# A Mamba and mixture-of-experts kernel: one pair of y additions moved from VectorE to ScalarE and GpSimd, two small products as transposes, statistics in later slots

## The reference

```python
x = x + layernorm(mamba(layernorm(x)))
x = x + layernorm(moe(layernorm(x)))

def mamba(x):                       # 512 channels, 16 states
    x_in, z = split(x @ W_in)
    u = silu(causal_conv4(x_in) + conv_b)
    dt, B, C = split(u @ W_xproj)
    delta = softplus(dt @ W_dt + b_dt)
    h = exp(delta * A) * h_before + delta * u * B    # for each channel and state n
    y = sum over n of h[n] * C[n]
    return ((y + D_skip * u) * silu(z)) @ W_out

def moe(x):                         # 8 experts of 128, top 2; a shared one of 256
    coef = softmax(x @ router), all but the two largest set to 0
    routed = sum over e of coef[e] * ((silu(x @ gate[e]) * (x @ up[e])) @ down[e])
    return routed + (silu(x @ s_gate) * (x @ s_up)) @ s_down
```

## Time and profile before

| | before |
|---|---|
| median of 3 runs | 2335.7 us (2333.97 to 2335.87) |
| the profiled execution | 2333.0 us, its span 2331.2 us |
| granted TensorE clock, mean over the span | 0.945 of full speed |
| DVE scans (L836), 1024 | 1261.1 us busy, 1267 ns each |
| DVE y additions (L846), 896 | 621.5 us busy, 735 ns each |
| GpSimd d_bu (L1103), 512 | 1202.2 us busy, 2359 ns each |
| ScalarE decays (L633), 1024 | 699.6 us busy, 691 ns each |
| TensorE transposes of h (L465), 4096 | 607.3 us busy |
| the page's 40 slices | VectorE 9 tenths in all but the first and the last two |

### The profile page before, as it was taken

The page is one execution under the profiler, slowest core; times in us unless marked ns, Lnnn a source line. Parts: engine busy times, 40 slices in busy tenths (PEclk is TensorE's granted clock), DMA queues, the critical chain, the costliest instruction groups (busy, mean ns, idle before and its releaser), DMA issues. The chain is left out here.

```text
span 2331.2 us, 30455 instructions
## 1 busy us (share of the span) xinstructions
PE 2070.9 (89%) x9280; PEld 1347.3 (58%) x9280; DVE 2155.3 (92%) x3056; ACT 1644.8 (71%) x2488; POOL 1963.8 (84%) x1625
## 2 busy tenths in 40 slices
PE   7678989999898999989899999998989989997978
PEld 4355665656566565655656566565656656565654
DVE  4999999999999999999999999999999999998950
ACT  5656877777777676777777777777768777775632
POOL 4677998989989898998989899898988989798844
PEclk8659999999999999999999999999999999998979
DMA  5111212211122121112211121121122111111201
GB/s 144 33 44 37 71 55 60 59 55 55 56 64 64 51 68 51 56 57 63 64 51 59 60 60 55 60 59 56 50 67 61 55 60 50 55 56 46 71 20 46
DMA packets 92995, 134.28 MB, mean 58 GB/s; under 512 B 12048, under 2 KB 43024, under 8 KB 92832
## 3 DMA queue, kind: packets, MB, share of 16 engines
q1 hardware_dynamic: 92832, 132.34, 18.4%
HBM read 123.13 MB, written 9.18 MB: 57 GB/s over the span
## 5 line engine op out<-in xcount | busy, mean ns | idle before, releaser
L836 DVE TENSOR_TENSOR_SCAN h<-d_a,carry,d_bu 128x512 f32<-128x512 f32 x1024 | 1261.1, 1267 | 47.0 <-ACT d_a L633 38.4
L1103 POOL TENSOR_TENSOR d_bu<-delta_u,b_rows 128x1024 f32<-128x1024 f32 x512 | 1202.2, 2359 | 4.4 <-issue 0.2
L633 ACT ACTIVATE d_a<-delta,a_neg 128x512 f32<-128x512 f32 x1024 | 699.6, 691 | 499.0 <-DVE h L836 493.9
L465 PE MATMUL ht<-ident,h 128*128 128x128 f32 x4096 | 607.3, 293 | 100.9 <-DVE y_t L846 94.3
L465 PEld LDWEIGHTS ht<-ident,h 128*128 128x128 f32 x4096 | 503.5, 150 | 333.6 <-issue 123.3
L846 DVE SCALAR_TENSOR_TENSOR y_t<-ht,c_t,y_t 128x512 f32<-128x512 f32 x896 | 621.5, 735 | 2.2 <-PE ht L465 1.5
L540 PE MATMUL ring<-x_t,w_gate_sb 128*128 128x512 f32 x640 | 327.8, 638 | 21.7 <-ACT delta L798 17.9
L567 PE MATMUL dn<-w_down_sb,up_hidden 128*128 128x256 f32 x1280 | 302.9, 379 | 1.7 <-POOL up_hidden L1166 1.7
L547 PE MATMUL ring<-x_t,w_up_sb 128*128 128x512 f32 x640 | 292.5, 600 | 11.9 <-ACT silu_gate L732 11.8
L1161 POOL TENSOR_TENSOR up_hidden<-silu_gate,up_hidden 128x512 f32<-128x512 f32 x160 | 204.3, 1277 | 110.8 <-ACT up_hidden L736 79.6
L567 PEld LDWEIGHTS dn<-w_down_sb,up_hidden 128*128 128x128 f32 x1280 | 236.0, 190 | 60.0 <-issue 31.8
(11 more groups left out here) (127 smaller groups left out, 2029.3 us busy)
## 6 DMA issues: line engine op xcount, KB each, us to landing
b_rows<-b_rows_hbm SPq DMA_DIRECT2D x256, 256.0 KB, 3.4
coef_rows<-coef_rows_hbm SPq DMA_DIRECT2D x128, 256.0 KB, 3.5
xa<-L_attn_x_in SPq DMA_DIRECT2D x16, 512.0 KB, 5.0
xr<-L_attn_x_in SPq DMA_DIRECT2D x16, 512.0 KB, 5.1
out<-xr SPq DMA_DIRECT2D x15, 512.0 KB, 2.9
w_in_sb<-L_attn_W_in_in SPq DMA_DIRECT2D x1, 1024.0 KB, 6.3
w_gate_sb<-L_ffn_experts_gate_in SPq DMA_DIRECT2D x2, 512.0 KB, 4.9
w_up_sb<-L_ffn_experts_up_in SPq DMA_DIRECT2D x2, 512.0 KB, 5.5
```

Of the source, the lines that this page charges most:

```text
L465: last = nc.tensor.transpose(HT[q % HTS][:, j * P:(j + 1) * P], H[:, (NS * c + n) % HS, j, a * P:(a + 1) * P], IDN[:, :])
L633: nc.scalar.activation(DA[i % DAS][:, :], DL[:, r, j, :], ACT.Exp, scale=ANEG[:, j, n:n + 1]).then_inc(ex.sem, 1)
L836: nc.vector.tensor_tensor_scan(H[:, (NS * s + n) % HS, j, :], DA[(n * J + j) % DAS][:, :], BU[:, (2 * n + j // 2) % 4, j % 2, :], CARRY[:, ...
L1103: nc.gpsimd.tensor_tensor(BU[:, (2 * n + h) % 4, :, :], DU[:, 2 * h:2 * h + 2, :], BB[:, n % 2, :].unsqueeze(1).to_broadcast([P, 2, T]), A ...
```

## The change

Tiles 14 and 15 are no longer added by VectorE. ScalarE scales each into one of the two buffers `UP`, and GpSimd adds both at once to `YT`. TensorE's tiles 16 and 17 wait for the ScalarE copies (`y_side`), VectorE's tiles 18 and 19 for the sum (`y_sum`), and so do the up copies of blocks 2 and 3, which write `UP`. The matmuls with the identity of `CF_PE` and `CT_PE` become transposes. Three entries of the statistics' table move: two `bn_stats` from slots 26 and 36 to 32 and 42, `XA_MEAN` from 42 to 46.

```diff
-        scan, add_c, carry = stage("scan", NS * J), stage("add_c", (NS - 2) * NT), stage("carry_s", NS)
+        y_side, y_sum = stage("y_side", 2), stage("y_sum", 1)
+        scan, add_c, carry = stage("scan", NS * J), stage("add_c", (NS - 2) * NT - 2), stage("carry_s", NS)
-        XA_STATS, XA_MEAN, XA_RSTD, XA_NORM, XT_PE, XT_ACT = (16, 16, 26, 36), 42, 47, 50, 61, 62
+        XA_STATS, XA_MEAN, XA_RSTD, XA_NORM, XT_PE, XT_ACT = (16, 16, 32, 42), 46, 47, 50, 61, 62
+        SIDE_SLOT = 20
+        SIDE_Q = ADDS[SIDE_SLOT]
         def added(c, q):
...
+            if q in SIDE_Q:
+                return y_side.sem, y_side.at(c, q - SIDE_Q[0] + 1)
-            return add_c.sem, add_c.at(c, q - NT + 1)
+            return add_c.sem, add_c.at(c, q - NT + 1 - (2 if q > SIDE_Q[1] else 0))
...
-                        last = nc.tensor.matmul(bank[0:E, a * P:(a + 1) * P], COEF[:, a, :],
-                                                IDN[:, :], start=True, stop=True)
+                        last = nc.tensor.transpose(bank[0:E, a * P:(a + 1) * P], COEF[:, a, :], IDN[:, :])
...
-                        last = nc.tensor.matmul(ring_bank("ct", 0)[:, a * NS:(a + 1) * NS],
-                                                XD[ROW_C:ROW_C + NS, o, a * P:(a + 1) * P],
-                                                IDN[ROW_C:ROW_C + NS, ROW_C:ROW_C + NS],
-                                                start=True, stop=True)
+                        last = nc.tensor.transpose(ring_bank("ct", 0)[:, a * NS:(a + 1) * NS],
+                                                   XD[ROW_C:ROW_C + NS, o, a * P:(a + 1) * P],
+                                                   IDN[ROW_C:ROW_C + NS, ROW_C:ROW_C + NS])
...
+            def side_state(c, r, q):
+                n, a = q // NT, q % NT
+                act.wait_ge(ht_full.sem, ht_full.at(c, q + 1))
+                act.wait_ge(hf.sem, hf.at(c - 1, up_used(1)))
+                act.wait_ge(y_sum.sem, y_sum.at(c - 1))
+                nc.scalar.activation(UP[:, q - SIDE_Q[0], :], HT[q % HTS][:, :], ACT.Copy,
+                                     scale=CT[:, r, a, n:n + 1]).then_inc(y_side.sem, 1)
...
+                    if with_scan and t == SIDE_SLOT:
+                        for q in SIDE_Q:
+                            side_state(s, r, q)
...
+                        if f // 2 == 1 and exists(lo):
+                            act.wait_ge(y_sum.sem, y_sum.at(s))
                         nc.scalar.activation(UP[:, f % 2, :], ring_bank("up", f)[:, :], ACT.Copy)\
...
-                dve.wait_ge(*added(c, q - NT))
+                if q - NT in SIDE_Q:
+                    dve.wait_ge(y_sum.sem, y_sum.at(c))
+                else:
+                    dve.wait_ge(*added(c, q - NT))
...
-                        if with_scan and q >= NT:
+                        if with_scan and q >= NT and q not in SIDE_Q:
                             add_state(s, r, q)
...
+            def side_sum(c):
+                a = SIDE_Q[0] % NT
+                pool.wait_ge(y_side.sem, y_side.at(c))
+                pool.wait_ge(*added(c, SIDE_Q[1] - NT))
+                nc.gpsimd.tensor_tensor(YT[:, a:a + 2, :], YT[:, a:a + 2, :],
+                                        UP[:, :, :], ALU.add).then_inc(y_sum.sem, 1)
...
+                    if with_scan and t == SIDE_SLOT + 2:
+                        side_sum(s)
```

## The result

The changed kernel has a median of 2340.03 us (2339.31 to 2341.73, 12 runs), the kernel before 2334.6 beside it (12 runs). The ratio is 1.0025, 95% interval [1.0017, 1.0032]. The change made the kernel 5.4 us slower.

A forecast was written before the change was run, and what follows sets the result against it. The bound was a loop of VectorE, ScalarE's copy and GpSimd's run releasing the next slot 4. With D -0.37 a chunk takes 138.3, 0.8 longer; 14 chunks less hidden parts give plus 9.5, 2345 us, range 2321 to 2352.

The forecast's parts named there:

- The additions and the room on ScalarE and GpSimd: Slots 20 to 21: VectorE saves 1.30 us a chunk, 20.8 at most; ScalarE's copies and GpSimd's 2.36 addition cost nothing.
- The late tiles: TensorE's tiles 16 and 17, behind ScalarE's copies, start 0.64 us later; with the clock low VectorE stalls about 0.5.
- low twice: TensorE clock at 1.2 GHz for both stretches of slots 21 to 24: D about -0.85, taken for about half the chunks.
- D: VectorE's lead in us left after the late tiles 16 and 17; forecast average -0.37 a chunk.
- low once: Clock low for one stretch of slots 21 to 24: D 0.1; in every chunk, as rival, 2338 us, chance 0.2.
- The aggregates' wait: GpSimd's rstd of x waits up to 0.9 us for VectorE's moved aggregates, within the run that sets slot 4.
- the drawn loop: VectorE from slot 4 to late additions, then GpSimd's run to the next slot 4's d_bu: 137.9 - D a chunk.
- The transposes and the places of the bn_stats: Transposes save 0.43 us each at slots 20 and 48, off any path; moved bn_stats cost VectorE nothing in sum.
- The sum: A chunk takes 138.3, 0.8 longer; 11 us over 14 chunks, less 1 to 2 hidden: plus 9.5, median 2345.
- The rival with the clock up: TensorE's clock stays up or is low too briefly: D near 1.2, loop 136.7, 2322.7 us; chance 0.32.

The follow-up runs named there:

- experiment with TensorE kept busy: Changed kernel plus nine matmuls of the identity, read by nobody, filling TensorE's idle ahead of the coefficients; copies stay behind the decay: 2315.0 us.
- the copies first: Changed kernel with ScalarE's two copies in slot 20 issued ahead of the decay of slot 22: 2313.9 us; with all statistics in their old slots too, 2309.3.
- the copies first and the aggregates back: Changed kernel with the copies ahead of the decay and the aggregates back in slot 42, bn_stats staying in 32 and 42: 2312.4 us.
- pair with TensorE kept busy: Changed kernel with nine unread identity matmuls ahead of the coefficients, statistics in new slots, 2315.0 us, or in old slots, 2326.1 us.

## Why the prediction was right, and where it was off

The sign and the range were right: slower, 2340 in 2321 to 2352. The time was forecast at 2345, 5 too much: 9.3 slower, where 5.4 was measured. By its steps:

*The additions and the room on ScalarE and GpSimd.* Right. The copies start at 1330.51, behind the decay, as worked out; the decays aren't late; the sum fits into the hole.

*The late tiles.* Right in mechanism and nearly in size. 2.09 idle before tile 16, as forecast. The clock falls in all twelve chunks and stays low twice in six of them, forecast as in all, and twice in about half. That half was assumed and not worked out, and the average D rests on it, so here the forecast had luck. At the scan of slot 47 a chunk low once is 0.22 ahead of before's chunk 8 (96.66 against 96.88 from slot 4) and one low twice 0.91 behind (97.79). The forecast had a lead D of 0.1 and -0.85. The experiment with TensorE kept busy shows that it is the clock that makes the lateness cost, and the one with the copies first that the lateness makes the clock cost.

*The aggregates' wait.* Right: 0.93 to 0.95 measured, "up to 0.9" forecast. The loop came out at 137.67 and 138.81, forecast 137.8 and 138.75 (137.9 - D). Slots 2 and 4 wait for GpSimd, as the drawn loop says. Done alone in the kernel before, the move costs 3.8 us.

*The transposes and the places of the bn_stats.* Right: nothing that can be told, where the clock is in the same state. With the copies first, VectorE reaches slot 47 in 95.45 with the new slots and in 95.53 with the old ones. With late copies, TensorE kept busy and the clock low at the same place, it is 97.49 (new, chunk 9) and 97.51 (old, chunk 5).

*The sum.* The term that was off is what stands outside the chunks, put at nothing. The steady chunk is 0.73 longer (138.38 less 137.65), close to the 0.8 of the forecast, and the 13 chunks from 1 to 13 took 9.2 more. But the stretch up to chunk 1's first scan is 1.7 shorter (170.9 against 172.6), and what follows the last scan 1.8 shorter (95.7 against 97.5). 9.2 + 1.2 for chunks 14 and 15, less 1.7 and 1.8, is the span's 6.9. I had counted a loss in 14 chunks, less what they hide (9.5), and everything outside them at nothing; measured are 10.4 lost in chunks 1 to 15 and 3.5 won outside them. That is 2.6 of the 5 us. Another 1.1 is the median of the kernel before, 2334.6 beside the changed one and not 2335.7. The last 1.5 comes from the profiled executions: that of the kernel before lay 1.6 below its median, that of the changed kernel at it. In chunk 0 there is no expert layer and TensorE isn't packed, which fits the additions coming off at full value there, but no run tried it. That the tail is shorter was seen and not traced.

*The rival with the clock up* was priced at 2322.7; it came out as 2315.0. The loop was put at 136.7 and took 136.4 (D is 1.4 and not 1.2), and the chunk before at 137.46, where the mean over chunks 2 to 12 was 137.65: not only the four chunks low twice were longer than 137.30, but also chunks 4, 7 and 10, by 0.4 to 0.5.

*The Trainium skill's advice* ("TensorE: Matmul & The Clock Gate", Part 1) says: "For modeling, the ramp penalty is <1% of a typical kernel span; don't fit to a specific cold count." I read that as leaving it out, which is more than the sentence says. Here keeping the clock up is worth 25 us of 2340, 1.07%, in the changed kernel, and 0.1% in the one before. The figure is of the right order, but leaving the penalty out would have given 2322.7 and the wrong sign.

**Which part costs what** can't be said as a sum. With the clock up, or with the copies first, the exchange of two additions gains some 20 us, measured with the new slots, and 4.6 more with the old ones. That is the price of the statistics' new places, and 0.5 a chunk of it is GpSimd's wait for the aggregates. With the copies last, the falls of the clock take the gain, and what the old slots give back from slot 47 on is mostly lost before it, so that the whole differs by 1.6 us, within the measurement.

## What to carry to other kernels

When work moves to an idle engine, look at what it stands behind in that engine's order, and not only at whether the engine has room: here the copies waited behind a decay, and so for a scan that they don't need, and moving them ahead of that decay was worth 26 us. A consumer's cover has to be counted against all that uses it up at once: a late release alone was free, a low TensorE clock alone cost 2 us, both together 25. And a statistic or a sum that is moved into a stall of its own engine may still be late for the engine that reads it.

## What the runs showed of the hardware that I had not expected

TensorE's clock settles into a rhythm with the loop. In the changed kernel chunks 4 to 11 alternate without exception between 137.6 to 137.7 (low once) and 138.8 (low twice). In the kernel with the copies first and the aggregates back, the clock falls in every chunk from 2 to 14, each time 52.3 to 53.4 us after the chunk's first scan, and chunks 4 to 13 take 136.53 to 136.62. In the pair with TensorE kept busy, the kernel whose clean chunk is 0.4 us shorter has twice the falls at slots 21 to 24 in its trace, more of the long falls over the end of a chunk, and is 11 us slower. So two kernels that differ by a few tenths of a microsecond in a chunk can't be compared by their whole times alone; chunks in the same clock state can.
